# Attention and expert layer on one core: the order of the first projection, of its row transfers, and of batch 1's projection

## What is computed

```
h = layernorm(x)
y = causal_attention(h Wq, h Wk, h Wv) + attention(h Wcq, ctx Wck, ctx Wcv)   # 16 heads of 8 channels, ctx 4 x 64 x 64
x = x + y Wp
h = layernorm(x)
x = x + shared_expert(h) + sum over the 8 best of 32 experts of weight * expert(h)
```

## Time and profile before

| | us |
|---|---|
| median of 3 runs | 213.03 (212.35 to 213.05) |
| the profiled execution | 212.95 |
| its span on the core | 211.1 |
| TensorE busy | 193.0 |
| VectorE busy | 163.8 |
| ScalarE busy | 140.7 |
| GpSimd busy | 95.5 |

### The profile page before, as it was taken

One profiled execution on the slowest core, in us unless ns is written; L12 is line 12 of the kernel. 1 busy time (PEld: TensorE's weight loads), 2 busy tenths in 40 slices (PEclk: granted clock), 3 DMA queues, 4 the chain that ended last, 5 costly groups with the idle time before them and its releaser, 6 DMA issues.

```text
span 211.1 us, 4012 instructions
## 1 busy us (share of the span) xinstructions
PE 193.0 (91%) x1239; PEld 139.6 (66%) x1251; DVE 163.8 (78%) x377; ACT 140.7 (67%) x275; POOL 95.5 (45%) x149
## 2 busy tenths in 40 slices
PE   7967988998999999898998886999999999999993
PEld 2635755766766767665765654778888888887662
DVE  2889994667688987987666799675788878887882
ACT  3457776778789888787786754754676566555571
POOL 7799881242182657448455053244255332220020
PEclk9999999999999999999999999699999999999997
DMA  4365423222342234101111100000033000000003
GB/s 117 86 150 138 111 71 75 43 70 75 89 94 68 71 83 114 39 0 40 40 38 37 37 0 2 3 0 0 2 75 79 17 2 0 0 3 0 0 0 99
DMA packets 20433, 10.39 MB, mean 49 GB/s; under 512 B 11881, under 2 KB 18542, under 8 KB 20414
## 3 DMA queue, kind: packets, MB, share of 16 engines
q1 hardware_dynamic: 19290, 9.24, 17.7%
q0 software_dynamic: 672, 0.69, 1.3%
q10 hardware_dynamic: 452, 0.23, 0.5%
HBM read 4.51 MB, written 0.52 MB: 24 GB/s over the span
## 4 chain that ended last, share of the span: by engine, by line
PE 65%; DVE 12%; issue 8%; ACT 8%; POOL 4%; DMA 1%; POOLq 1%; DVEq 0%; ACTq 0%
PE psum L1282 12%; PE psum L1283 11%; PE psum L1284 11%; PE psum L1385 5%; PE psum L1613 3%; PE psum L1458 3%; PE psum L1470 3%; PE psum L1480 3%; PE psum L1440 2%; PE psum L1435 2%; PE psum L1384 2%; PE psum L1421 2%; PE psum L1405 2%; PE psum L1444 1%; PE psum L1463 1%
## 5 line engine op out<-in xcount | busy, mean ns | idle before, releaser
L869 ACT ACTIVATE gate<-psum,bias_cols 128x512 f32<-128x512 f32 (+2 forms) x35 | 23.5, 674 | 31.8 <-PE psum L1284 31.7
L756 ACT ACTIVATE probs<-psum 128x512 f32<-128x512 f32 x64 | 36.9, 598 | 2.8 <-PE psum L1440 1.4
L1225 DVE SCALAR_TENSOR_TENSOR gated<-psum,bias_cols,gate 128x512 f32<-128x512 f32 x32 | 24.0, 749 | 11.4 <-ACT gate L869 10.9
L607 POOL TENSOR_TENSOR w_ffn_lo<-w_ffn,w_ffn_hi 128x384 fp32r<-128x384 f32 x17 | 20.7, 1216 | 25.8 <-ACT w_ffn_hi L770 25.8
L1282 PE MATMUL psum<-xT_hi,w_ffn_hi 128*128 128x512 f32 x66 | 27.1, 410 | 0.0
L1283 PE MATMUL psum<-xT_lo,w_ffn_hi 128*128 128x512 f32 x66 | 26.5, 401 | 0.0
L1284 PE MATMUL psum<-xT_hi,w_ffn_lo 128*128 128x512 f32 x66 | 26.0, 394 | 0.0
L1385 PE MATMUL psum<-key_blocks,query_rows 96*128 96x512 f32 x48 | 23.0, 522 | 0.3 <-issue 0.3
L1238 DVE TENSOR_TENSOR hid<-gated,psum 128x512 f32<-128x512 f32 x32 | 21.8, 683 | 1.6 <-PE psum L1613 0.6
L665 POOL TENSOR_TENSOR hid_lo<-hid,hid_hi 128x512 fp32r<-128x512 f32 x9 | 11.6, 1293 | 24.5 <-ACT hid_hi L876 24.5
L631 POOL TENSOR_SCALAR_AFFINE_SELECT probs<-probs 128x512 f32<-128x512 f32 x16 | 10.2, 640 | 27.1 <-ACT probs L756 27.0
(11 more groups left out here) (179 smaller groups left out, 475.6 us busy)
## 6 DMA issues: line engine op xcount, KB each, us to landing
query_rows<-queries SPq DMA_DIRECT2D x46, 64.0 KB, 2.0
key_rows<-keys SPq DMA_DIRECT2D x39, 32.0 KB, 1.9
w_ffn<-in_L_ffn_Wg SPq DMA_DIRECT2D x16, 64.0 KB, 1.9
w_ffn<-in_L_ffn_Wu SPq DMA_DIRECT2D x16, 64.0 KB, 2.1
w_ffn<-in_L_ffn_Wd SPq DMA_DIRECT2D x16, 64.0 KB, 2.1
...
```

Of the source, the lines that this page charges most:

```text
L607: ins = pool.tensor_tensor(w_ffn_lo[:, k, :, :], w_ffn[:, k, :, :], w_ffn_hi[:, k, :, :].bitcast(F32), ALU.subtract).then_inc(ffn_lo, 1)
L756: act.activation(probs[:, i % 2, c, :], bank(B_ST + c % 2), ACT.Exp, scale=SCALE).then_inc(exp_done, 1)
L869: act.activation(gate[rows_of(n), n % 3, part], psum[of, B_GATE + n % 2, part], ACT.Silu, bias=bias_cols[of, BIAS_GATE + u:BIAS_GATE + u + ...
L1225: dve.scalar_tensor_tensor(out=gated[:, n % 3, :], in0=bank(B_UP + n % 2), scalar=bias_cols[:, BIAS_UP + u:BIAS_UP + u + 1], in1=gate[:, n ...
```

## The change

TensorE: two idle products fewer behind the turn of ctx, the context keys ahead of the turn of x, the two idle products behind the turn of biases; project(0) becomes project_first. Behind it eight idle products, the biases of the experts, the turn of x of batch 1, five idle products, natural(0). Of batch 1 only keys and queries are projected there, into B_OUT (bank 6); the cross queries and the values are a tail of step 0, in bank 7. All other projection tails move one step back. natural(1) is split: tile 0 before scores(0, 0), context and tile 1 behind scores(0, 1). context_values moves behind scores(0, 3) and waits for batch 1's queries to be split.

VectorE: head mask and identities first, the context copy before norm(0), bias columns before split_x(0); the three splits of batch 0 together, then both statistics, norm(1); split_x(1) and values(0) in maxima(0), expand(2) in maxima(1); the splits of batch 1 behind maxima(1), cvalues at the end of step 0. ScalarE: three more transfers (context keys of group 1), round_x(1) behind the first expansions, keys and queries of batch 1 rounded ahead of shift(0), the four norms at the end of step 0. GpSimd: another order of memsets and key transfers, the memset of cvalue in two halves, and expand_ctx(2) and (3) wait for VectorE's blocks of steps 2 and 3. SP: the context keys of group 3, and place_batch_1.

```diff
@@ -307,10 +307,10 @@
         TAIL = ("y_turn", "project", "x2_turn", "router")
-        tail_at = {0: [("x_pair", FIRST_BATCHES)]}
+        tail_at = {0: [("cross_values", 1)], 1: [("x_pair", FIRST_BATCHES)]}
         for b in range(FIRST_BATCHES, BATCH):
-            tail_at[2 * b - 3] = [("keys_queries", b)]
-            tail_at[2 * b - 2] = [("cross_values", b)]
+            tail_at[2 * b - 2] = [("keys_queries", b)]
+            tail_at[2 * b - 1] = [("cross_values", b)]
         late_at = {}
@@ -354,14 +354,15 @@
-            if b < FIRST_BATCHES:
+            if b == 0:
                 return bank(B_QKC + n, SEQ)
             half = n % 2
-            return psum[:, B_MISC, SEQ * half:SEQ * (half + 1)]
+            to = B_OUT if b == 1 and n < 2 else B_MISC
+            return psum[:, to, SEQ * half:SEQ * (half + 1)]
...
-            half = b >= FIRST_BATCHES
+            half = b >= 1
             return psum[:, B_VALUE, SEQ * half:SEQ * (half + 1)]
@@ -425,6 +426,19 @@
                     head_mask[0:ROWS, j:j + 1])
+        def place_batch_1(sp):
+            sp.wait_ge(qkc_rounded, 4)
+            sp.wait_ge(qkc_split, 4)
+            place_keys(sp, 1, 0)
+            place_keys(sp, 1, 1)
+            sp.wait_ge(qkc_rounded, 6)
+            sp.wait_ge(qkc_split, 6)
+            for g in range(GROUPS):
+                place_queries(sp, 1, g)
+                if g + 2 < GROUPS:
+                    place_keys(sp, 1, g + 2)
@@ -493,7 +507,11 @@
                 place_queries(sp, 0, g)
-            place_batch(sp, 1)
+            sp.wait_ge(ck_rounded, 1)
+            sp.wait_ge(ck_split, 1)
+            sp.wait_ge(ckey_rows_set, 1)
+            place_ctx_keys(sp, 3)
+            place_batch_1(sp)
@@ -540,32 +558,31 @@
+            pool.memset(value[:, :, :, D:D + 1], 1.0).then_inc(zeroed, 1)
             first_rstd(0)
+            pool.memset(ckey_rows[:, :, :].bitcast(F32), -1.0).then_inc(ckey_rows_set, 1)
             chain(pool.memset(causal[:, :, :], 0.0))
...
                                pattern=[[0, GROUP], [-1, P]], channel_multiplier=1).then_inc(have_causal, 1)
-            pool.wait_ge(x_normed, NORM_GROUPS[0][1])
-            pool.memset(value[:, :, :, D:D + 1], 1.0).then_inc(zeroed, 1)
-            pool.memset(ckey_rows[:, :, :].bitcast(F32), -1.0).then_inc(ckey_rows_set, 1)
-            chain(pool.memset(cvalue[:, :, :, :], 0.0))
-            first_rstd(1)
             pool.wait_ge(ck_rounded, 1)
...
             place_ctx_keys(pool, 0)
+            chain(pool.memset(cvalue[:, 0:BATCH // 2, :, :], 0.0))
+            first_rstd(1)
             pool.wait_ge(qkc_rounded, 1)
             pool.wait_ge(qkc_split, 1)
+            pool.wait_ge(rows_set, 1)
             place_keys(pool, 0, 1)
+            place_keys(pool, 0, 2)
             first_rstd(2)
-            place_ctx_keys(pool, 1)
-            place_keys(pool, 0, 2)
+            place_ctx_keys(pool, 2)
+            place_keys(pool, 0, 3)
             pool.wait_ge(have_rstd, 3)
+            chain(pool.memset(cvalue[:, BATCH // 2:BATCH, :, :], 0.0))
             pool.memset(cvalue[0:CTX, :, :, D:D + 1], 1.0).then_inc(zeroed, 1)
...
             pool.memset(cvalue[CTX:P, :, :, 32 + D:32 + D + 1], 1.0).then_inc(zeroed, 1)
-            place_ctx_keys(pool, 2)
-            place_keys(pool, 0, 3)
-            place_ctx_keys(pool, 3)
@@ -577,6 +594,7 @@
             pool.wait_ge(zeroed, 3)
+            pool.wait_ge(v_blocks_set, 6)
             expand_ctx(2)
@@ -640,6 +658,7 @@
                     pool.wait_ge(selected, 2)
+                    pool.wait_ge(v_blocks_set, 8)
                     expand_ctx(3)
@@ -717,29 +736,32 @@
                 bias = ORDER[n][1]
-                act.wait_ge(m_qkc, 3 * b + max(n, b >= FIRST_BATCHES) + 1)
+                act.wait_ge(m_qkc, 3 * b + max(n, b >= 1) + 1)
                 act.activation(projected(b, n, 0), product_bank(b, n), ACT.Identity,
...
             round_x(0)
-            for b in range(FIRST_BATCHES):
-                if b == 0:
-                    act.wait_ge(in_w_cqv, 32)
-                    act.copy(w_qkv_hi[:, 2:4, :], w_qkv[:, 2:4, :]).then_inc(w_qkv_rounded, 1)
-                    act.wait_ge(have_bias_cols, 1)
-                    act.wait_ge(m_ck, 1)
-                    act.activation(ckeys[:, 0, :], bank(B_CK, CTX_KEYS), ACT.Identity,
-                                   bias=bias_cols[:, BIAS_CK:BIAS_CK + 1]).then_inc(ck_rounded, 1)
-                for n in range(3):
-                    round_qkc(b, n)
-                if b == 0:
-                    act.wait_ge(rows_set, 1)
-                    act.wait_ge(qkc_rounded, 3)
-                    place_queries(act, 0, 0, (0, 2))
-                    round_x(1)
-                    expand(0)
-                    expand_ctx(0)
-                    expand(1)
+            act.wait_ge(in_w_cqv, 32)
+            act.copy(w_qkv_hi[:, 2:4, :], w_qkv[:, 2:4, :]).then_inc(w_qkv_rounded, 1)
+            act.wait_ge(have_bias_cols, 1)
+            act.wait_ge(m_ck, 1)
+            act.activation(ckeys[:, 0, :], bank(B_CK, CTX_KEYS), ACT.Identity,
+                           bias=bias_cols[:, BIAS_CK:BIAS_CK + 1]).then_inc(ck_rounded, 1)
+            for n in range(3):
+                round_qkc(0, n)
+            act.wait_ge(rows_set, 1)
+            act.wait_ge(qkc_rounded, 3)
+            place_queries(act, 0, 0, (0, 2))
+            act.wait_ge(ck_rounded, 1)
+            act.wait_ge(ck_split, 1)
+            act.wait_ge(ckey_rows_set, 1)
+            place_ctx_keys(act, 1)
+            expand(0)
+            expand_ctx(0)
+            round_x(1)
+            expand(1)
+            round_qkc(1, 0)
+            round_qkc(1, 1)
@@ -803,10 +825,6 @@
                 exps(i, (0,))
-                if i == 0:
-                    act.wait_ge(have_neg_mean, 1)
-                    for t in range(*NORM_GROUPS[2]):
-                        norm(t)
                 if i + 1 < STEPS:
@@ -829,6 +847,10 @@
                     tail(name, b)
+                if i == 0:
+                    act.wait_ge(have_neg_mean, 1)
+                    for t in range(*NORM_GROUPS[2]):
+                        norm(t)
                 if i:
@@ -947,16 +969,18 @@
             dve.memset(fill[:, :], 0.0).then_inc(fill_set, 1)
-            stats_of(0)
-            norm(0)
             dve.wait_ge(have_ident, 1)
...
             dve.tensor_tensor(head_mask[:, :], head_mask[:, :], ident[:, SHIFT_ROW:ROWS], ALU.add).then_inc(have_mask, 1)
+            dve.tensor_copy(ident_bf[:, :], ident[:, :])
+            dve.tensor_copy(ident_r[:, :], ident[:, :]).then_inc(have_idents, 1)
+            stats_of(0)
             dve.wait_ge(have_ctxT2, 1)
...
                             ).then_inc(have_ctxT, 1)
+            norm(0)
             dve.wait_ge(w_qkv_rounded, 1)
@@ -971,7 +995,7 @@
                 bias = ORDER[n][1]
-                dve.wait_ge(qkc_rounded, 3 * b + max(n, b >= FIRST_BATCHES) + 1)
+                dve.wait_ge(qkc_rounded, 3 * b + max(n, b >= 1) + 1)
                 dve.scalar_tensor_tensor(out=projected(b, n, 1), in0=product_bank(b, n),
@@ -987,11 +1011,10 @@
-            split_x(0)
-            stats_of(1)
             dve.wait_ge(t_bias, 1)
...
                             bank(B_BIAS, 4)).then_inc(have_bias_cols, 1)
+            split_x(0)
             dve.wait_ge(w_qkv_rounded, 2)
@@ -999,15 +1022,11 @@
                                      op0=ALU.add, op1=ALU.subtract).then_inc(ck_split, 1)
-            split_qkc(0, 0)
+            for n in range(3):
+                split_qkc(0, n)
+            stats_of(1)
+            stats_of(2)
             norm(1)
-            split_qkc(0, 1)
-            split_qkc(0, 2)
-            stats_of(2)
-            split_x(1)
-            dve.tensor_copy(ident_bf[:, :], ident[:, :])
-            dve.tensor_copy(ident_r[:, :], ident[:, :]).then_inc(have_idents, 1)
-            values(0)
@@ -1020,7 +1039,7 @@
-            def maxima(i, outputs=-1):
+            def maxima(i, outputs=-1, ahead=-1):
@@ -1044,12 +1063,15 @@
+                    split_x(1)
+                    values(0)
                     dve.wait_ge(m_nat, 2)
                     tile_1()
-                    values(1)
                     dve.wait_ge(m_nat, 3)
...
                     return
+                if ahead >= 0:
+                    expand(ahead)
                 dve.wait_ge(m_nat, 3 * i + 2)
@@ -1150,17 +1172,15 @@
             maxima(0)
-            for n in range(3):
-                split_qkc(1, n)
+            expand(1)
+            expand_ctx(1)
+            maxima(1, ahead=2)
+            split_qkc(1, 0)
+            split_qkc(1, 1)
             rest = slice(*NORM_GROUPS[2])
...
                                      op0=ALU.mult, op1=ALU.mult).then_inc(have_neg_mean, 1)
-            expand(1)
-            expand_ctx(1)
-            maxima(1)
-            expand(2)
-            cvalues()
             for i in range(STEPS):
@@ -1172,6 +1192,8 @@
```

(58 more changed lines are left out.)

## The result

| | before | changed |
|---|---|---|
| median, first measurement | 213.04 (4 runs) | 215.34 (214.3 to 215.92, 4 runs) |
| ratio, 95% interval | 1 | 1.011 [1.0063, 1.0158] |
| median, second measurement (e12 below) | 212.99 (17 runs) | 214.30 (213.25 to 215.29, 12 runs) |
| ratio, 95% interval | 1 | 1.0058 [1.0029, 1.0087] |
| the profiled execution | 212.95 | 214.96 |

The change is a loss: 2.3 us in the first measurement, 1.3 us in the second, which has more runs and the narrower interval. The forecast was +0.8 us with a range up to 215.1, so the sign was right, the size was not: the first median lies 0.2 above the range, the second inside it, 0.5 above the forecast. The two profiled executions differ by 2.1 us of span, and that is what is explained here.

The account below looks back on a forecast made before the run. VectorE was taken to bound up to about 23 us, TensorE's chain behind it. A lead of 0.8 us and 1.7 for one more tail gave +0.9 on 212.95: 213.85, taken as 213.8, range 212.2 to 215.1.

Parts of the forecast that it names:

- First projection: Batch 0's key product, freed of mask and copies ahead, starts 0.5 us earlier than 8.03, within 0 to 0.9.
- The last split at 10.0: VectorE's last split of batch 0's projection ends at 10.0 us instead of 11.38.
- a rival near 12 and 22 us: TensorE gaps there halve its granted clock over 2 to 3 us of matmuls: +1.3, total 215.1; chance 0.05.
- Natural(0) at 14.55: First natural scores start at 14.55 us against 14.69, after norm(1), the turn of x and five idle products.
- Late norm: Rival: GpSimd's rstd of batch 1 comes late behind key transfers; natural(0) at 15.2, total 214.5; chance 0.16.
- Steps 0 and 1: TensorE bound from 23.2; uncovered context_values (1.16) and batch 1 products (1.17) eat the gain; x_pair split 0.8 us ahead.
- The port at 19.4: Half the cvalue memset beside VectorE's expand(1) and expand_ctx(1) costs 0.1 us, between 0 and 0.6.
- Steps 2 to 6: One more keys-and-queries tail costs 1.7 us, giving +0.9 at the first turn behind projections; transfers stay covered.
- The sum: At the first turn behind the projections -0.8 + 1.7 = +0.9 us, which reaches the end: 213.85, taken as 213.8.

Follow-up runs that it names:

- e12: The changed kernel again with no edit: 214.30 us (12 runs), ratio 1.0058.
- e3: The changed kernel with GpSimd's memset of ckey_rows moved back behind the causal mask: 213.75 us (7 runs), ratio 1.0025.
- e13: The kernel before again with no edit, for a second profile: 212.41 us (one run).
- e1: The changed kernel's start up to natural(0) with the old steps, batch 1 projected whole: 214.27 us (10 runs), ratio 1.0063.
- e6: e1 with the memset of ckey_rows behind the causal mask: 213.17 us (10 runs), ratio 0.9984.
- e2: The kernel before up to natural(0), with the changed order of steps from there on: 218.86 us, ratio 1.0275.
- e4: The changed kernel with two idle products between the context keys' product and the turn of x of batch 0: 214.52 us (5 runs), ratio 1.0057.
- e8: e2 with four idle products ahead of the context scores of step 2: 214.28 us (11 runs), ratio 1.0062.
- e11: The start of e10 with the changed kernel's own steps: 213.68 us (12 runs), ratio 1.0037.
- e7: The kernel before with only GpSimd's memset of ckey_rows moved early, its wait for normalized x gone: 213.90 us (10 runs), ratio 1.0037.
- e9: e6 with VectorE's identity casts behind batch 0's statistics and three idle products instead of five ahead of natural(0): 213.01 us (10 runs), ratio 0.998.
- e10: e6 with two idle products more ahead of batch 0's turn of x and three instead of five ahead of natural(0): 213.91 us (12 runs), ratio 1.0045.

## Why the prediction was right and wrong

**First projection: the step that failed.** The forecast took the first product at 7.5; it came at 8.39. I had written a range from "0 if the idle products still hold TensorE" to 0.9 earlier, and looked at the idle products and the bias work, not at what the re-ordered GpSimd queue does beside VectorE's norm. The diff shows it: the memset of ckey_rows moved from behind the wait for x_normed to ahead of it. I weighed the port for the half memset of cvalue at 19.4 and took 0.1; I didn't ask the same for the first one. Where it is taken away (e3) the first product starts at 7.25, better than forecast. The Trainium skill's page "SBUF — State Buffer", section "Who interferes with whom", says that a VectorE instruction in a two-port mode and a GpSimd instruction shut each other out for a whole instruction, and lists tensor_scalar, which the norm is, among those that can enter such a mode. The norm of 1.48 us beside the memset of 0.96 agrees with it, the norm of 0.60 beside a bf16 memset (e13) does not.

**The last split at 10.0.** It ended at 11.22 + 0.48 = 11.70. Of the 1.7 us 0.9 are the late first product, the rest the products at 0.21 instead of 0.12 us. In e3 the splits end at 8.82 + 0.87 = 9.69. The prediction priced the clock as a rival near 12 and 22 us (0.05, +1.3), but held that the start was safe, because before had a gap of 1.70 us ahead of natural(0) without harm. The price was right, the place and the chance were not.

**Natural(0) at 14.55.** It came at 15.96, +1.41, and this one term is the whole miss of the profile: what follows cost 0.87 us more than before where the forecast had 1.04. Norm(1) was to end at 12.95 and ended at 13.88 + 0.64 = 14.52. That natural(0) would start directly behind idle products was right, with 0.2 us to spare: ScalarE's five transfers held it until 14.71, not 12.95, and its key blocks end at 14.81 + 0.91 = 15.72. The first eight were thought of as filling only; at the lower level they ended behind the norm in e12.

**Late norm.** It didn't happen: GpSimd waited for VectorE's var_eps (12.41 + 0.17) and had the rstd at 13.45, before VectorE asked for it at 13.88.

**Steps 0 and 1.** Counted from natural(0), forecast and measured: scores(0, 0) 5.10 and 4.85; turn(1) 8.35 and 8.38; scores(1, 0) 13.05 and 12.95; turn(2) 15.15 and 14.78; scores(2, 0) 19.20 and 19.29; the end of the x_pair split 20.35 and 20.14 (35.41 + 0.69 = 36.10). Against before, where the reader of that bank ended 35.67 - 14.69 = 20.98 behind natural(0), it is 0.84 ahead; the forecast had 0.8 by absolute times, with natural(0) itself 0.14 ahead. The two uncovered pieces, context_values and the products of batch 1, are where the gain of step 0 went: e1 has scores(0, 0) at 23.34 and scores(1, 0) at 28.56, the changed kernel 20.81 and 28.91.

**The port at 19.4.** The half memset came at 20.59 in the changed kernel, when the expansion beside it was nearly done, and that one kept 0.60: nothing was lost. In e6 it came first and an expansion took 0.36 longer. The 0.1 between ends of 0 and 0.6 was fair.

**Steps 2 to 6.** Forecast +1.7 for one tail more; measured turn(3) to turn(7) 25.55 against 23.85: +1.70. Six other profiles of the new steps (e2, e3, e4, e8, e11, e12) give 25.50 to 25.54, those of the old ones (e1, e6, e7, e9, e10, e13) 23.81 to 23.87. The transfers of batches 2 and 3 were covered, as argued.

**The sum.** Forecast +0.9 = -0.14 (start) + 1.04; measured at turn(7) +2.14 = +1.27 + 0.87. That the second median lies inside the range is no success of the sum: its range was to hold a start between 13.9 and 15.2, and the two starts read in the changed kernel are 15.96 and 16.36.

**What stays open.** The medians fall less far apart than the profiles: the changed kernel is 1.3 us behind in e12, and e3 and e11, whose profiled executions are level with the kernel before (212.78 and 212.93), have medians 0.8 and 1.1 us above it. Two things that vary between executions bear on this.

The first is the level of the start. The record gives each timed run its mean granted clock. Take only the runs with 0.994 or more:

| | runs with a mean granted clock of 0.994 or more |
|---|---|
| before (42 runs) | 212.26 to 212.78 |
| e8, start of before (9) | 214.22 to 214.41 |
| e7, start of before, memset early | 213.06 to 213.21 (4), 214.27 to 214.62 (4) |
| changed, both measurements | 213.25 (1), 214.18 to 214.41 (3) |
| e1 | 213.65 to 213.87 (4), 214.21 and 214.34 (2) |
| e3 | 212.27 (1), 213.75 to 214.05 (3) |
| e4 | 213.22 (1), 214.52 (1) |
| e6 | 212.11 to 212.18 (4), 213.12 to 213.75 (4) |
| e9 | 211.96 to 212.31 (4), 212.96 to 213.15 (4), 213.76 (1) |
| e10 | 212.61 and 212.77 (2), 213.62 to 214.00 (7) |
| e11 | 212.62 to 212.93 (4), 214.21 to 214.67 (4) |

The start of before gives one narrow group. Every other start spreads, mostly into two groups 0.8 us or more apart (e1 by 0.3). The profiled executions of e6 and e11, products 0.12 apart, belong to the lower groups (212.18, 212.93), that of e10, 0.21 apart in most of them, to the upper (214.00), that of e9, half and half, to the middle one (212.96). e1's (213.77) is in its lower group although its level was low until 10.8; there the norm is long in every execution. So the groups are most likely executions whose level came up early or late; that is read from four profiles and not shown for each run. It also says where the chance is: not in the start of before, but in both the early memset alone (e7) and the new start without it (e6). The lower group of e6 lies below every run of the kernel before, and the changed kernel's one lower run is 0.7 us above the middle of the other's group in its session (212.53), close to the forecast.

The second is a fall of the clock near 134 us, in a part of the kernel that no edit touches. The kernel before has a granted clock of 0.50 at 134 to 136 us in its first profile and 1.00 in e13, and from turn(7) to the end of the span takes 151.27 and 150.73. The changed kernel has the same pair, 151.23 and 150.73 (e12), so the comparison of the first two profiles is a fair one. In e4 and e8 the fall is longer and this part takes 152.78 and 152.83: their profiled times, 215.26 and 216.36, are 1.5 to 2 us longer for it, and not for their starts. How often each kernel meets it isn't settled; it blurs the medians of all.

No version beat the kernel before: e6 and e9 lie at 0.998 with 1 inside both intervals.
